# Two expert layers: one program block per layer, with the tokens in two groups

## What is computed

```python
logits = xf @ Wg.T + bg                       # 8 experts
probs = softmax(logits); tp, ti = top_k(probs, 2)
w = sum(one_hot(ti, 8) * tp[..., None], axis=1)
h = gelu(einsum('td,efd->tef', xf, W1) + b1)  # 512 hidden features; 256 in layer 1
y = einsum('tef,edf->ted', h, W2) + b2        # no b2 in layer 1
out = einsum('ted,te->td', y, w)
x = x + gb * (x_normed + out)
```

## Time and profile before

| what | value |
|---|---|
| median of 3 timed runs | 2325.47 us (2324.65 to 2326.64) |
| the profiled execution, its time | 2310.59 us |
| its span (first to last instruction) | 2308.0 us |
| PE busy | 1623.6 us, 70% |
| DVE busy | 1372.0 us, 59% |
| ACT busy | 1117.9 us, 48% |
| POOL busy | 576.7 us, 25% |
| DMA | 136.48 MB, mean 59 GB/s |

### The profile page before, as it was taken

The page is one execution under the profiler, slowest core; times in us unless marked ns, Lnnn a source line. Parts: engine busy times, 40 slices in busy tenths (PEclk is TensorE's granted clock), DMA queues, the critical chain, the costliest instruction groups (busy, mean ns, idle before and its releaser), DMA issues. The chain is left out here.

```text
span 2308.0 us, 34300 instructions
## 1 busy us (share of the span) xinstructions
PE 1623.6 (70%) x11520; PEld 935.1 (41%) x11520; DVE 1372.0 (59%) x3362; ACT 1117.9 (48%) x2900; POOL 576.7 (25%) x637
## 2 busy tenths in 40 slices
PE   7899898989933099503599999999999730604730
PEld 4378676877832099502212222222222330504620
DVE  5555454545567032137899999999997176713323
ACT  3176565757631044202148888888888640201210
POOL 3123222222255500275100000000100043371046
PEclk9799999999965599856679999999999965657975
DMA  4711111111100177411301000010100000014632
GB/s 147 294 36 27 28 36 28 29 26 36 36 4 32 53 227 230 128 52 43 106 16 31 16 24 22 17 30 16 31 16 3 1 2 1 14 51 120 177 107 73
DMA packets 85229, 136.48 MB, mean 59 GB/s; under 512 B 17520, under 2 KB 56304, under 8 KB 84912
## 3 DMA queue, kind: packets, MB, share of 16 engines
q1 hardware_dynamic: 72708, 98.85, 15.2%
q0 software_dynamic: 11744, 34.49, 4.5%
q10 hardware_dynamic: 588, 0.81, 0.1%
HBM read 72.89 MB, written 45.09 MB: 51 GB/s over the span
## 5 line engine op out<-in xcount | busy, mean ns | idle before, releaser
L1685 DVE TENSOR_REDUCE q_max<-s_ps 128x1 f32<-128x1024 f32 x512 | 598.8, 1217 | 11.8 <-PE s_ps L1577 5.2
L1667 ACT ACTIVATE probs<-s_ps 128x512 f32<-128x512 f32 x1024 | 533.9, 603 | 140.7 <-PE s_ps L1598 140.5
L1577 PE MATMUL s_ps<-k_stack,q_stack 64*128 64x512 bf16 x1024 | 358.4, 404 | 21.9 <-PEq L93 11.4
L1598 PE MATMUL s_ps<-q_stack,k_stack 64*128 64x512 bf16 x1024 | 315.1, 384 | 20.9 <-ACT probs L1667 14.4
L1612 PE MATMUL o_ps<-probs,v_aug 128*32 128x512 f32 x2048 | 273.2, 606 | 0.7 <-ACT probs L1667 0.7
L846 POOL TENSOR_TENSOR probs<-probs,p_rsum 128x512 f32<-128x512 f32 x128 | 133.1, 1040 | 373.4 <-DVE p_rsum L825 373.4
L781 ACT ACTIVATE probs<-s_biased,s_min 128x128 f32<-128x128 f32 x512 | 199.5, 395 | 44.7 <-DVE s_min L819 44.7
L1598 PEld LDWEIGHTS s_ps<-q_stack,k_stack 64*128 64x128 bf16 x1024 | 78.3, 94 | 336.5 <-ACT probs L1667 285.5
L819 DVE CUSTOM_DVE_ANT_0 s_biased<-score_ps,nbias 128x128 f32<-128x128 f32 x512 | 117.6, 286 | 70.5 <-PE score_ps L707 69.6
L707 PE MATMUL score_ps<-k_pad,q_bd 128*128 128x128 f32 x1024 | 144.2, 284 | 0.0
L1577 PEld LDWEIGHTS s_ps<-k_stack,q_stack 64*128 64x128 bf16 x1024 | 76.9, 94 | 133.9 <-DVE q_max L1685 121.1
(11 more groups left out here) (299 smaller groups left out, 2938.8 us busy)
## 6 DMA issues: line engine op xcount, KB each, us to landing
moe0b_wblock<-in_L_ffn_blocks SPq DMA_DIRECT2D x39, 578.0 KB, 4.1
moe_rows<-zero_rows POOLq DMA_DIRECT2D x6, 2880.0 KB, 28.3
moe1b_wblock<-in_L_ffn_blocks SPq DMA_DIRECT2D x39, 256.0 KB, 3.0
v_shift<-v_tiles SPq DMA_DIRECT2D x32, 256.0 KB, 3.1
v_shift<-v_tiles SPq DMA_DIRECT2D x32, 224.0 KB, 3.6
qk_parts_dram<-qk_parts SPq DMA_DIRECT2D x16, 384.0 KB, 2.4
q_stack<-qk_parts_dram SPq DMA_DIRECT2D x180, 32.0 KB
k_stack<-qk_parts_dram SPq DMA_DIRECT2D x180, 32.0 KB
```

The source lines that it names most:

```text
L1577: mm = nc.tensor.matmul(s1[u % 2][:, c * CH:(c + 1) * CH], qs[head_rows(m), quad % 4, j, qt * P:(qt + 1) * P], ks[head_rows(m), quad % 4, ...
L1598: nc.tensor.matmul(bank_of("exp", 4 * k + pos)[:], ks[head_rows(m), quad % 4, j, kt * P:(kt + 1) * P], qs[head_rows(m), quad % 4, j, half ...
L1667: nc.scalar.activation(pr[:, k % 2, HEADS[pos], :], bank_of("exp", n)[:], ACT.Exp).then_inc(sm["exp"], 1)
L1685: v.tensor_reduce(mx[:, quad % 2, col:col + 1], s1[u % 2][:], AX.X, ALU.max).then_inc(sm["maxed"], 1)
```

## The change

The three blocks of an expert layer become one. The engines' programs of the blocks and of the gather stand in a new class `ExpertBlocks`, and each is called at the end of that engine's program in the norm stage.

The tokens are in two groups of two batches, (0, 2) and (2, 4). Each group has its own region of `moe_rows`, its own scatter semaphore, its own table and its own 4096 / 256 + 7 = 23 blocks, 46 in all. `tabulate` runs once per group, right behind the placement of the group's last batch. SP starts the loads of a group when its table is there and its scatters have landed. POOL scatters all four batches, then waits for the stores of group 0's blocks and gathers its 32 tile rows, then the same for group 1. DVE combines all chunks behind its last block, since `chunk_of_block` gives None throughout with two groups. SP reads the table for four blocks at once. The PSUM banks of the routing serve the blocks too, for which PE waits until all four batches are placed. `moe_rows` grows to 36352 rows, which the zero fill rounds up to 38016, with 11 DMAs in pieces of 3 rows in place of 6 in pieces of 5.

```diff
+GROUPS = ((0, 2), (2, 4))
+GROUP_BLOCKS = tuple(2 * (b1 - b0) * T // BR + E - 1 for b0, b1 in GROUPS)
+NBK = sum(GROUP_BLOCKS)
+ROWS = E * B * T + len(GROUPS) * (E - 1) * BR
+ZR, ZREP = 3, 9
+ZDMAS = -(-ROWS // (P * ZR * ZREP))
+ROWS_ALL = ZDMAS * P * ZR * ZREP
...
                     if M and b >= 5:
                         M.place(dve, b - 5)
+                        if b - 4 in [b1 for _, b1 in GROUPS]:
+                            M.tabulate(dve, [b1 for _, b1 in GROUPS].index(b - 4))
                 if M:
-                    M.tabulate(dve)
+                    X.vector(dve)
...
                 if M:
                     for b in range(B):
                         M.scatter(pool, N2, b)
-                    M.wait_scattered(pool)
+                    X.gpsimd(pool)
...
-            for n in range(ROWS // P // ZR // 9):
-                part = rows[:, 9 * n * ZR * D:9 * (n + 1) * ZR * D].rearrange("p (k z) -> p k z", k=9)
-                pool.dma_start(part, bc(zero[:], 1, 9)).then_inc(cleared, 16)
+            for n in range(ZDMAS):
+                size = ZREP * ZR * D
+                part = rows[:, n * size:(n + 1) * size].rearrange("p (k z) -> p k z", k=ZREP)
+                pool.dma_start(part, bc(zero[:], 1, ZREP)).then_inc(cleared, 16)
...
+class ExpertBlocks:
...
+    def sync(self, sp):
+        nc, M, K = self.nc, self.M, self.K
+        rows, experts = {}, {}
+        for j in range(NBK + LATE):
+            if j < NBK:
+                g = sum(j >= f for f in FIRST_BLOCK) - 1
+                k = j - FIRST_BLOCK[g]
+                if k == 0:
+                    sp.wait_ge(M.tabled, g + 1)
+                if k % 4 == 0:
+                    n = min(4, GROUP_BLOCKS[g] - k)
+                    _, got = nc.values_load_multi_w_load_instructions(
+                        M.table[0:1, g, 0, k:k + n], engines=(mybir.EngineType.SP,), min_val=0, max_val=E - 1)
+                    experts.update(zip(range(j, j + n), got))
+                    _, got = nc.values_load_multi_w_load_instructions(
+                        M.table[0:1, g, 1, k:k + n], engines=(mybir.EngineType.SP,), min_val=0, max_val=ROWS - BR)
+                    rows.update(zip(range(j, j + n), got))
+                e = experts.pop(j)
+                if k == 0:
+                    M.wait_scattered(sp, g)
+                if j >= XB:
+                    sp.wait_ge(self.turned, j - XB + 1)
...
+                if j >= WBUF:
+                    sp.wait_ge(self.y_out, j - WBUF + 1)
...
+            if j >= LATE:
+                k = j - LATE
+                sp.wait_ge(self.y_out, k + 1)
...
+    def gpsimd(self, pool):
+        M = self.M
+        for g, (b0, b1) in enumerate(GROUPS):
+            done = FIRST_BLOCK[g] + GROUP_BLOCKS[g]
+            for i in range(YB):
+                pool.wait_ge(self.stored[i], 16 * len(range(i, done, YB)))
+            for t in range(b0 * TPB, b1 * TPB):
+                for c in range(2):
+                    self.nc.gpsimd.indirect_dma_start(
+                        self.yg[:, t, c, :], None, self.K.moe_rows,
+                        bass.IndirectOffsetOnAxis(ap=M.slot[:, c, t:t + 1], axis=0)
+                    ).then_inc(self.gathered[t // CPT], 16)
...
+        pe.wait_ge(M.shifted, B)
+        pe.wait_ge(M.placed, B)
+        turn(0)
+        for j in range(NBK + 1):
+            if j + 1 < NBK:
+                turn(j + 1)
+            if j < NBK:
+                hidden(j)
+            if j >= 1:
+                out_rows(j - 1)
...
+        for c in range(combined, NCH):
+            combine(c)
```

More of the change, by code:

```diff
@@ L43 @@
 BR = 256
-SPAN = B * T
-NBK = 2 * B * T // BR + E - 1
-ROWS = E * SPAN + (E - 1) * BR
-ZR = 5
+GROUPS = ((0, 2), (2, 4))
+GROUP_BLOCKS = tuple(2 * (b1 - b0) * T // BR + E - 1 for b0, b1 in GROUPS)
+FIRST_BLOCK = tuple(sum(GROUP_BLOCKS[:g]) for g in range(len(GROUPS)))
+NBK = sum(GROUP_BLOCKS)
+NBKP = -(-max(GROUP_BLOCKS) // 4) * 4
+GROUP_ROW = tuple(E * b0 * T + g * (E - 1) * BR for g, (b0, b1) in enumerate(GROUPS))
+ROWS = E * B * T + len(GROUPS) * (E - 1) * BR
+ZR, ZREP = 3, 9
+ZDMAS = -(-ROWS // (P * ZR * ZREP))
+ROWS_ALL = ZDMAS * P * ZR * ZREP
 STEPS_OF = T * B // BR
@@ L186, in double_norm_stage @@
         N2 = Norm(nc, K, name + "b", K.nat, hat2, st)
-        banks = [K.ps(f"{name}_ps{i}", [P, CPT, P], st) for i in range(4)]
+        banks = X.banks if M else [K.ps(f"{name}_ps{i}", [P, CPT, P], st) for i in range(4)]
         (aff_in, scaled, shifted) = K.sems(st, name, "affine_in", "scaled", "shifted")
@@ L278, in last_norm_stage @@
         M.router_buffers(st)
+        X = M.blocks_of(st)
         N = Norm(nc, K, name, K.nat, hat, st)
-        banks = [K.ps(f"{name}_ps{i}", [P, CPT, P], st) for i in range(4)]
+        banks = X.banks
         (aff_in,) = K.sems(st, name + "w", "affine_in")
@@ L301, in _ @@
                         M.place(dve, b - 2)
-                M.tabulate(dve)
+                        if b - 1 in [b1 for _, b1 in GROUPS]:
+                            M.tabulate(dve, [b1 for _, b1 in GROUPS].index(b - 1))
+                X.vector(dve)
             @block.gpsimd
@@ L1017, in place, with tabulate @@
         v.tensor_copy(self.slot[:, :, ts], self.place_f[:]).then_inc(self.placed, 1)
-    def tabulate(self, dve):
+    def tabulate(self, dve, g):
         v, step = self.nc.vector, self.step
-        base, marks = self.steps[:, 0:E], self.steps[:, E:E + STEPS_OF]
-        number = self.steps[:, E + STEPS_OF:]
+        b0, b1 = GROUPS[g]
+        n, marked, G = GROUP_BLOCKS[g], (b1 - b0) * T // BR, len(GROUPS) * E
+        base, marks = self.steps[:, g * E:(g + 1) * E], self.steps[:, G:G + marked]
+        number = self.steps[:, G + STEPS_OF:G + STEPS_OF + n]
         blocks, first, upto = (self.nb[:, i, :] for i in range(3))
-        passed, spent = self.le[:, 0], self.le[:, 1]
-        expert, row, rest = (self.tf[:, i, :] for i in range(3))
-        step(dve, v.tensor_tensor(first, self.cum[:, NT, :], base, ALU.subtract))
-        step(dve, v.tensor_tensor(self.over[:], bc(first, 2, STEPS_OF), bc(marks, 1, E), ALU.is_gt))
-        step(dve, v.tensor_reduce(blocks, self.over[:], AX.X, ALU.add))
+        passed, spent = self.le[:, 0, 0:n], self.le[:, 1, 0:n]
+        expert, row, rest = (self.tf[:, i, 0:n] for i in range(3))
+        step(dve, v.tensor_tensor(first, self.cum[:, b1 - 1, TPB, :], base, ALU.subtract))
+        over = self.over[:, :, 0:marked]
+        step(dve, v.tensor_tensor(over, bc(first, 2, marked), bc(marks, 1, E), ALU.is_gt))
+        step(dve, v.tensor_reduce(blocks, over, AX.X, ALU.add))
         g4 = self.gt[:, 0, :].rearrange("p (a b) -> p a b", a=E)
@@ L1038, in tabulate @@
         step(dve, v.tensor_tensor(rest, number, rest, ALU.subtract))
-        step(dve, v.tensor_scalar(rest, rest, float(BR), None, ALU.mult))
-        step(dve, v.scalar_tensor_tensor(out=row, in0=expert, scalar=float(SPAN), in1=rest, op0=ALU.mult,
+        step(dve, v.tensor_scalar(rest, rest, float(BR), float(GROUP_ROW[g]), ALU.mult, ALU.add))
+        step(dve, v.scalar_tensor_tensor(out=row, in0=expert, scalar=float((b1 - b0) * T), in1=rest, op0=ALU.mult,
                                          op1=ALU.add))
         step(dve, v.tensor_scalar(expert, expert, float(E - 1), None, ALU.min))
-        v.tensor_copy(self.table[:], self.tf[:, 0:2, :])
+        v.tensor_copy(self.table[:, g, :, 0:n], self.tf[:, 0:2, 0:n]).then_inc(self.tabled, 1)
     def scatter(self, pool, N, b):
@@ L1048, in scatter @@
         N.wait_normalised(pool, (b + 1) * TPB)
+        g = [b < b1 for _, b1 in GROUPS].index(True)
         for t in range(b * TPB, (b + 1) * TPB):
```

387 lines of the change are left out of this document (189 added, 198 removed).

## The result

The changed kernel takes 2341.64 us in the median (2337.16 to 2343.98), the kernel before 2324.65 us beside it; the ratio is 1.0073, with a 95% interval of 1.0054 to 1.0092. The forecast was 2197 us.

A forecast was written before the change was run, and what follows sets the result against it. PE was taken to bound layer 0's blocks, SP layer 1's, POOL scatter and gather. Layer 0 -58.2, layer 1 -75.0, start +4.6 make -128.6 us: median 2196.9 us, range 2160 to 2238.

The forecast's parts named there:

- Step 1: Head of each layer: blocks start after half the scatter, first x load earlier, -49.2 us (layer 0) and -48.8 us (layer 1).
- Step 2: Layer 0's blocks: 23 + 23 instead of 39, seven more at 3.73 us each, +26.1 us.
- Step 4: Blocks beside POOL's scatter: x loads land later, +5 us (layer 0), +4 us (layer 1); slower POOL descriptor work stays hidden.
- step 3: Layer 1's blocks: SP reads four table entries at once, 2.63 us a block, +10.3 us including seven more blocks.
- Rival F: Kernel slower than before: x loads beside POOL's DMAs land very late, a landing of 14 us giving 2350 us; chance 0.02.
- rival C: SP's table loads aren't merged: a 5.3 us piece of SP work, together +50 us, 2247 us; chance 0.10.
- Steps 5 and 6: End of each layer: POOL waits on the stores itself, -1.5 us; only half the gather left at the end, -40.3 us.
- Step 7: Way out of the merged stage: more sets of semaphores to clear, +1.7 us (layer 0) and +1.3 us (layer 1).
- Step 8: Zero fill at the rms stage: 38016 rows instead of 34560, +4.6 us; 0 to 10 us as bounds.

The follow-up runs named there:

- the changed kernel with the pause: Changed kernel plus one POOL fill of 128x512, waited for, behind each indirect DMA that lies beside blocks; 2218.88 us, ratio 0.9548 to the kernel before.

## Why the forecast was wrong, step by step

The steps from the first scatter to the next stage, in us, from the starts of the rows named; the third column is the changed kernel with the pause (2220.1 us span):

| step | before | changed | with pause |
|---|---|---|---|
| layer 0: first scatter to first x load | 91.3 | 43.1 | 43.0 |
| to the first result | 12.9 | 47.2 | 18.9 |
| first to last result | 139.6 | 203.2 | 166.8 |
| to the next stage's first operation | 101.6 | 65.8 | 65.2 |
| layer 1: first scatter to first x load | 90.7 | 42.3 | 42.3 |
| to the first result | 10.4 | 45.5 | 19.1 |
| first to last result | 108.1 | 169.8 | 139.5 |
| to the end of the span | 92.7 | 53.8 | 54.4 |

*Step 1*, -49.2 and -48.8: right for the load (-48.2 and -48.4), as the earlier trace rows gave it. What stands behind it was taken at nothing, and that is where 34 and 35 us of it were lost.

*Step 2*, seven more blocks: 3.73 us each held wherever POOL was still, and with the pause 46 blocks took 27.2 us more than 39: right.

*Step 4* **is the one that failed.** It asked two things of work beside POOL's DMAs: whether the bytes fit, and whether DVE slows POOL. It never asked whether POOL slows the others, and put that at nothing without a row. Bytes were no problem (0.91 of the DMA engines with PE full), and the 5 + 4 us were, if anything, too much. The real price was 34.3 + 36.4 us in layer 0 (first result; first to last result less the 27.2 of step 2) and 35.1 + 30.3 in layer 1 (first result; first to last result against the kernel with the pause, which has step 3's cost in it too): about 136 us where 9 stood. The pause gave back 123 by the medians. Rival F had the right side with the wrong mechanism, late x loads; the x load of 767.05 was transposed 2.1 us later. The rows from which it could have been doubted are few: in the earlier trace rows the other engines are simply idle beside POOL's scatter from 742 on. DVE's work beside the first twenty-odd scatters was read only for what DVE does to POOL; that it ran at its usual pace says little, for by theory S it was using up instructions that it had.

*Step 3*, the table entries: the loads are merged (24 per source line, 0.30 us each in the steady stretch; rival C falls), but the term was mis-sized. 45 x 2.63 stood against 139.5 us with the pause, +31 instead of +10.3. With one group four blocks took 11.4 us, not 10.5, most likely because the fourth block's x load is late by more than the working allowed, and the next weight loads wait for its result. Both that value, 2.84, and the 3.10 with two groups and the pause (139.5 / 45) lie between the bounds given (2.19 to 3.27). Of the 21 us that the term fell short, 45 x (2.84 - 2.63) = 9.6 are this; the other 11 come with the two groups, and no run splits them further (with fills in place of the DMAs a block took 2.97).

*Steps 5 and 6*: group 0's gather lies amid the blocks, the last part is 32 DMAs long, and from the last result to group 1's first gather are 3.1 us instead of 4.3: right. *Step 7* was too small: behind the last gather layer 0's way out takes 4.7 us more (22.8 instead of 18.0), with the pause 4.2, not 1.7.

*Step 8*, zero fill, +4.6: the window attention begins 9.8 us later. ACT's first operation there, with the two groups and with one:

```profile
112.19 1.28 ACT L780 ACT_TABLE_LOAD   x1 [27.48 <-PEq L99]
```

```profile
105.79 1.28 ACT L780 ACT_TABLE_LOAD   x1 [24.20 <-PEq L99]
```

In the kernel before it was at 102.34. So 3.4 us come from pieces of 1.5 KB instead of 2.5 KB (same rows, ten DMAs instead of six), the bound that the forecast named, and 6.4 from the rows. These are differences of single profiles: with the same fill as in the changed kernel the other runs' lie between 110.6 and 113.2. In the four runs with pieces of 2.5 KB and 38400 rows it was at 106.1 to 107.8, so that the rows alone cost 3.7 to 5.5 us there, around the forecast's 4.6.

The kernel with the pause, layer 0's first load and first result:

```profile
765.75 0.36 SPq L1165 DMA_DIRECT2D moe_xin<-moe_rows  x1
...
784.71 0.42 DVE L1282 TENSOR_TENSOR moe_y<-moe_counts_ps,moe_wblock 128x256 f32<-128x256 f32 x1 [4.06 <-PE moe_counts_ps L1231]
```

It saves 88 us in the profile where the forecast had 129. By the medians it saves 104 (2322.72 to 2218.88): the forecast carried over that the median of before lies 14.9 us above its profile, while in the changed kernel and in this one the median lies 2 and 3 us below. The missing 41 of the profile: 21 in step 3; 15 before the first results (18.9 and 19.1 us instead of 12.9 and 10.4), most likely slow instructions left over from the unpaced half of the scatter; 6 behind the last results; 5 in the zero fill; 2 in small change; less 8, since the transfers cost next to nothing of the 9 us set aside.

## What to carry to other kernels

Before work is put beside a dense row of indirect DMAs, ask what the DMAs do to the other engines' instructions, not only whether bytes and buffers fit; a stretch in which the others idled is no row for that, and neither is one in which they ran a few dozen instructions. Look at instruction counts per stretch: engines that are all idle with "issue" as the reason, and a DMA share of 0.4, are short of instructions. Where it happens, half a microsecond of pause behind each indirect DMA costs little, as long as the DMAs still fit beside the work; unpaced overlap gave 9 us of 40 to 49.

## What the runs showed of the hardware

- Indirect DMAs of POOL 1.26 or 1.36 us apart slow the instructions of PE and SP to one per 0.7 to 1.4 us each; DVE's table operations of 0.18 us come up to 1.8 us apart (759.15 to 764.45; 0.2 at 737), and ACT shows only that it waits, mostly for PE. DMAs 1.54 us apart do it partly (PE 2.6 instructions per us, in layer 0's first stretch), 1.52 us apart hardly where they begin with no backlog (6.5 per us); 1.8 us apart not at all after a start of some 15 us. It sets in late: PE had some 45 passes first, and among SP's operations in layer 0 one of 0.7 us stands first in 739.5 to 741.1, 16 us behind the first scatter (min, median, max in ns; first and last start):

```profile
L1143 SPq SEQ_ASSERT  x4: 3/28/695, 739.5 to 741.1; - x4
```

- 8 rows do it as 128 do; 32 and 64 do too; 96 direct DMAs 0.53 us apart, and fills, don't.
- It lasts 5 to 8 us behind the last one, while POOL's drain behind the scatter of the kernel before is 5.28 us long.
- What it is inside the chip stays open. It isn't seen in the fetches: the 47 us from 767 to 814 have one fetch of instructions in the DMA queues' table. The Trainium skill (Runtime: NRT & Kernel Launch, "Instruction fetch mechanics") says that each engine has a store of instructions refilled in blocks of 256. A store of instructions would fit the late onset. But an engine whose block was late would by this rule stand still and then run on, while the trace shows one instruction at a time. Every execution here was recorded with its span and clock; whether recording takes part in it can't be told from these runs.
